# Attention over gathered rows: tying a body's gathers to the transposes of two bodies before

## The chip, the cores and the metric

The kernel runs on one core of one Trainium2 chip. The metric is the device time of one execution in microseconds (us), and a version is given by the median of its runs.

## What is computed

A graph of 6250 nodes and 100000 edges (sorted by receiving node) goes through a node update and two layers of attention over edges. The part that matters here is the attention of one layer:

```python
q = (x @ Wq + bq).reshape(n, H, C)          # n = 6250, H = 4, C = 32
k = (x @ Wk + bk).reshape(n, H, C)
v = (x @ Wv + bv).reshape(n, H, C)
e = (ea @ We).reshape(-1, H, C)             # 100000 edges
kj = k[src] + e
alpha = einsum('ehc,ehc->eh', q[dst], kj) / sqrt(C)
ex = exp(alpha - amax[dst])                 # softmax over the edges of a node
w = ex / (segment_sum(ex, dst)[dst] + 1e-16)
out = segment_sum((v[src] + e) * w, dst) + x @ Ws + bs
```

The kernel multiplies the projections into the queries beforehand, so that the attention works on the rows `x[src]` themselves: it gathers them, scores them against the queries of the receiving window, and sums the weighted rows.

## The kernel before

Edges are handled in tiles of 128. A **body** is four tiles (`QUAD`), and one attention stage has 224 bodies; there are two such stages, one for each layer (`attend_stage`). Each engine runs a loop whose round is eight bodies (`NS = 8`), written out body by body. All engines are coordinated by semaphores alone.

For body b the work is: SyncE loads the edge records of two bodies at a time (`part`, L1283), the queries and node codes of each body (L1305, L1306) and the edge codes (L1291). GpSimd gathers 4 x 128 rows of 128 floats by four indirect DMAs (L1326) into slot b mod 8 of the tile `ring`. TensorE turns the rows (`turn_rows`, L1340, four transposes) and puts the mask into the score bank (`mask_scores`, L1350). ScalarE copies the turned rows out of PSUM (`copy_rows`, L1411). TensorE scores them (`score`, L1358). VectorE finds the running maximum (L1460, L1463, L1467). ScalarE makes the weights (`weigh`, L1418, L1422). TensorE turns the weights (`turn_weights`, L1367), ScalarE copies them (`copy_weights`, L1429), TensorE multiplies them with the ring's rows (`gather_sums`, L1377) and VectorE adds the result to the sums (`add`, L1478).

The engines are staggered by hand. In step k TensorE does, in this order, the rows and mask of body k+2, the sums of body k, the scores of body k+2 and the weights' transposes of body k+1. ScalarE does `copy_rows` of k+2, `copy_weights` of k+1, `weigh` of k+2. VectorE does the small copy of k+2 (L1453), `add` of k, the maximum of k+2.

GpSimd has nothing else in these stages. Before the gathers of body b it waits for the edge records of b (`edge_in`) and for the sums of body b-8 (`summed`), which is when the slot of the ring is free again. So it may run up to six steps ahead of the transposes that read the rows. TensorE's matmuls signal `turned` (rows transposed), `scored`, `wt_ps` (weights transposed) and `summed`; counts that begin above zero are set by `sem_inc` at the start (L1391, L1392).

In the profile TensorE shows twice as many L1377, L1358 matmuls as the code writes, and L1340 and L1367 once each.

Of the kernel before, what the change touches and what calls it, by code (L numbers as in the profile page):

```python
# [33 lines left out]
NS = 8  # L34
# [167 lines left out]
def last_tiles(eng, m):  # L202

    return eng.value_load(m["atab"][0:1, 1, NWIN + 2:NWIN + 3], min_val=NWIN // TPR - 1, max_val=TCAP // TPR - 1)


def rounds(eng, m, step, begin=None, last_of=last_round, between=()):

    last, done = last_of(eng, m), 0
    for until, what in (*between, (last, None)):  # L210
        if what is None or until > done:
            with eng.Fori(done, until) as r:
                at = Round(eng, r)
                if begin:
                    begin(at, True)
                for k in range(NS):
                    step(at, k, NS)
        if what:
            what()
            done = until  # L220
    at = Round(eng, last)
    if begin:
        begin(at, False)
    for k in range(NS):
        step(at, k, NS - 1 - k)
# [986 lines left out]
def attend_stage(nc, m, layer):  # L1212
# [8 lines left out]
    with ExitStack() as c, ExitStack() as inner:  # L1221
# [36 lines left out]
        def xt_bank(k):  # L1258
            return bank[k % 2][:, 0:QE]

        def score_bank(k):
            return bank[2 + k % 2][:, 0:QE].rearrange("q (t e) -> q t e", t=QUAD)

        def wt_bank(k):
            return bank[4 + k % 2][:, 0:QE]

        def sum_bank(t):
            return bank[6 + t // 2][:, t % 2 * RW:(t % 2 + 1) * RW]

        def tiles_of(k, field, count=1):  # L1270
            here = field * NS + k % PART * QUAD * count
            return edge[:, k // PART, here:here + QUAD * count]

        def halves(at, c):
            return at.value(2 * NS, 2 * c)
# [39 lines left out]
        @block.gpsimd  # L1315
        def _(pool):
            pool.memset(codes[:, :, :, :], 1.0).then_inc(ready, 1)
            pool.memset(ring[:, :, :, FEAT:FEAT + 1], 1.0).then_inc(ready, 1)

            def step(at, k, left):  # L1320
                if k % PART == 0:
                    pool.wait_ge(edge_in[k // PART], at.turns(16, 0))
                pool.wait_ge(summed, halves(at, k + 1))
                pool.sem_inc(begun, 1)
                for t in range(QUAD):
                    pool.indirect_dma_start(  # L1326
                        out=ring[:, k, t, 0:FEAT], out_offset=None, in_=rows_of[:, :],
                        in_offset=bass.IndirectOffsetOnAxis(ap=tiles_of(k, 0)[:, t:t + 1], axis=0)
                        ).then_inc(rows_in[k], 16)

            rounds(pool, m, step, None, last_tiles)

        @block.tensor
        def _(pe):
            def turn_rows(at, body):

                k = body % NS
                pe.wait_ge(rows_in[k], at.turns(16 * QUAD, body))
                for t in range(QUAD):
                    last = pe.transpose(xt_bank(k)[:, t * P:(t + 1) * P], ring[:, k, t, 0:FEAT], ident[:, :])  # L1340
                last.then_inc(turned, 1)

            def mask_scores(at, body):

                k = body % NS
                pe.wait_ge(query_in[k % QS], at.value(2 * 64, 64 * (1 + body // QS)))
                pe.wait_ge(codes_in[k // PART], at.turns(16, body))
                for t in range(QUAD):

                    pe.matmul(score_bank(k)[:, t, :], nodes[:, k % QS, t, :], codes[:, k % QS, t, :], start=(t == 0),  # L1350
                              stop=False, skip_group_check=True)

            def score(at, body):

                k = body % NS
                pe.wait_ge(xt_there, at.body(body + 1))
                for t in range(QUAD):
                    last = pe.matmul(score_bank(k)[:, t, :], query[:, k % QS, t, :], x_t[k % 2][:, t * P:(t + 1) * P],  # L1358
                                     start=False, stop=True, skip_group_check=True)
                last.then_inc(scored, 1)  # L1360

            def turn_weights(at, body):

                k = body % NS
                pe.wait_ge(weighed, at.body(body + 1))
                for t in range(QUAD):
                    last = pe.transpose(wt_bank(k)[:, t * P:(t + 1) * P], weight[k % 2][:, t * P:(t + 1) * P], ident[:, :])  # L1367
                last.then_inc(wt_ps, 1)

            def gather_sums(at, k):  # L1370

                pe.wait_ge(wt_there, at.body(k + 1))
                pe.wait_ge(weights_in, at.body(k + 1))
                for half in (0, 2):
                    pe.wait_ge(added, at.value(NS * QUAD, QUAD * (k - 1 + NS) + half + 2))
                    for t in (half, half + 1):
                        last = pe.matmul(sum_bank(t), weight_t[k % 2][:, t * P:(t + 1) * P], ring[:, k, t, :], start=True,  # L1377
                                         stop=True)
                    last.then_inc(summed, 1)

            def step(at, k, left):
                if left >= 2:
                    turn_rows(at, k + 2)
                    mask_scores(at, k + 2)
                gather_sums(at, k)
                if left >= 2:
                    score(at, k + 2)
                if left >= 1:
                    turn_weights(at, k + 1)

            pe.sem_inc(summed, 2 * NS)  # L1391
            pe.sem_inc(scored, QS)  # L1392
            pe.wait_ge(ready, 5)
            begin = Round(pe, pe.snap(last_tiles(pe, m) * 0))
            for body in (0, 1):
                turn_rows(begin, body)
                mask_scores(begin, body)
                score(begin, body)
            turn_weights(begin, 0)
            rounds(pe, m, step, None, last_tiles)  # L1400

        @block.scalar
        def _(act):
            def copy_rows(at, body):

                k = body % NS
                act.wait_ge(turned, at.body(body + 1))
                if body >= 2:
                    act.wait_ge(scored, at.body(body - 1 + QS))
                    act.wait_ge(wt_ps, at.body(body - 1))  # L1410
                act.activation(x_t[k % 2][:, :], xt_bank(k), ACT.Copy).then_inc(xt_there, 1)  # L1411

            def weigh(at, body):

                k = body % NS
                act.wait_ge(shifted, at.body(body + 1 + NS))
                for t in range(QUAD):
                    last = act.activation(weight[k % 2][:, t * P:(t + 1) * P], score_bank(k)[:, t, :], ACT.Exp,  # L1418
                                          bias=run[:, k, t, STEPS - 1:STEPS])
                last.then_inc(weighed, 1)  # L1420
                act.wait_ge(changed, at.body(body + 1))
                act.activation(decay[:, k, :], change[:, k, :], ACT.Exp).then_inc(decayed, 1)  # L1422

            def copy_weights(at, body):

                k = body % NS
                act.wait_ge(wt_ps, at.body(body + 1))
                act.wait_ge(summed, halves(at, body - 1 + NS))
                act.activation(weight_t[k % 2][:, :], wt_bank(k), ACT.Copy).then_inc(wt_there, 1)  # L1429

            def step(at, k, left):
                if left >= 2:
                    copy_rows(at, k + 2)
                if left >= 1:
                    copy_weights(at, k + 1)
                if left >= 2:
                    weigh(at, k + 2)

            begin = Round(act, act.snap(last_tiles(act, m) * 0))
            copy_rows(begin, 0)  # L1440
            copy_rows(begin, 1)
            weigh(begin, 0)
            copy_weights(begin, 0)
            weigh(begin, 1)
            rounds(act, m, step, None, last_tiles)
# [500 lines left out]
```

## Time and profile before

| | us |
|---|---|
| median of 3 runs | 4399.23 |
| lowest, highest | 4367.18, 4400.29 |
| the profiled execution | 4405.89 |
| its span, first to last instruction | 4404.2 |
| granted TensorE clock, mean share of full | 0.775 |

The profile is of one execution. Its page gives busy times by engine, and views of the trace give groups of instructions, waits and an ordered list (the timeline). An engine row is the start in us from the start of the span, the duration, the engine, the line, the operation, tiles written<-read and the number merged; in brackets stands the idle time of the engine before it and what ended that. Of TensorE's matmuls the ends are modelled. "remote" is a wait whose release the profile could not assign to an instruction; "issue" is idle time before which nothing was waited for that the profile shows.

### The profile page before, as it was taken

What the parts mean: (1) busy time and instruction counts of PE and PEld (TensorE: products, weight loads), DVE (VectorE), ACT (ScalarE), POOL (GpSimd) and SP (SyncE); (2) the same over time, 40 slices, a digit from 0 to 9 for tenths busy, and PEclk for the clock granted to TensorE, in tenths of its full rate; (3) what the DMA queues carried; (4) which work ended last, traced back from release to release, by engine and by line L of the source; (5) the groups of instructions that cost most, each with busy time, mean ns of one, the idle gap of its engine ahead of it and who ended that gap; (6) DMA issues with size and microseconds to landing.
All of it is one profiled execution on the core that took longest, in us unless ns stands there. A gap on an engine that the chain in (4) does not pass through costs nothing. (4 is left out here: it accounts for less than half of the span.)

```text
span 4404.2 us, 85656 instructions
## 1 busy us (share of the span) xinstructions
PE 2949.7 (67%) x20523; PEld 2457.6 (56%) x20523; DVE 1843.2 (42%) x5924; ACT 1349.6 (31%) x4260; POOL 1920.7 (44%) x2203
## 2 busy tenths in 40 slices
PE   4567998466666666666667765666666666665676
PEld 2225998355555555555556544555565555555554
DVE  6464554233333333333335752333333333333357
ACT  1001443233333333333234432333333333332333
POOL 5200111555555555555552125555555555555522
PEclk5557999677777777777778987777777777777889
DMA  6985333232232223222233542222232223222220
GB/s 186 233 247 168 81 81 89 78 81 80 76 80 78 78 78 83 78 80 79 76 82 65 140 135 75 77 78 79 79 81 78 79 80 80 79 81 74 81 40 23
DMA packets 558920, 407.12 MB, mean 92 GB/s; under 512 B 229605, under 2 KB 526693, under 8 KB 558745
## 3 DMA queue, kind: packets, MB, share of 16 engines
q1 hardware_dynamic: 450840, 283.23, 22.9%
q0 software_dynamic: 58496, 122.80, 11.4%
q10 hardware_dynamic: 49536, 0.55, 0.6%
q8 instruction: 18, 0.29, 0.0%
q14 instruction: 30, 0.24, 0.0%
HBM read 333.73 MB, written 72.56 MB: 92 GB/s over the span
## 5 line engine op out<-in xcount | busy, mean ns | idle before, releaser
L1326 POOL DMA_INDIRECT a_ring<-xg,a_edge x1792 | 1690.3, 943 | 1498.8 <-issue 512.7
L1478 DVE SCALAR_TENSOR_TENSOR acc_all<-acc_all,a_decay,bank 128x130 f32 x1792 | 627.4, 350 | 1458.6 <-remote 906.5
L1377 PE MATMUL bank<-a_ring,a_weight_t 128*128 128x130 f32 x3584 | 684.4, 344 | 631.0 <-ACT a_weight_t L1429 330.5
L1358 PE MATMUL bank<-a_x_t,a_query 128*128 128x128 f32 x3584 | 707.7, 359 | 512.4 <-ACT a_x_t L1411 278.4
L1377 PEld LDWEIGHTS bank<-a_ring,a_weight_t 128*128 128x128 f32 x3584 | 571.6, 239 | 722.2 <-DVE acc_all L1478 359.0
L1358 PEld LDWEIGHTS bank<-a_x_t,a_query 128*128 128x128 f32 x3584 | 611.3, 257 | 593.1 <-ACT a_x_t L1411 320.9
L1429 ACT ACTIVATE a_weight_t<-bank 128x512 f32<-128x512 f32 x448 | 267.5, 597 | 1692.7 <-remote 777.8
L1418 ACT ACTIVATE a_x_t<-bank,a_run 128x128 f32<-128x128 f32 x1792 | 509.3, 371 | 271.2 <-DVE a_run L1463 211.4
L1460 DVE TENSOR_REDUCE a_bound<-bank 128x4 f32<-128x512 f32 x448 | 308.6, 689 | 424.3 <-issue 180.7
L1340 PE MATMUL bank<-ident,a_ring 128*128 128x128 f32 x1792 | 349.8, 331 | 37.3 <-DMA a_ring<-xg,a_edge 37.1
L1367 PE MATMUL bank<-ident,a_x_t 128*128 128x128 f32 x1792 | 364.1, 341 | 0.4 <-issue 0.4
L1411 ACT ACTIVATE a_x_t<-bank 128x512 f32<-128x512 f32 x448 | 273.9, 611 | 281.5 <-remote 210.6
L1340 PEld LDWEIGHTS bank<-ident,a_ring 128*128 128x128 f32 x1792 | 286.9, 179 | 38.5 <-DMA a_ring<-xg,a_edge 38.4
L1367 PEld LDWEIGHTS bank<-ident,a_x_t 128*128 128x128 f32 x1792 | 294.4, 183 | 0.7 <-issue 0.7
L517 PE MATMUL bank<-c_ring,c_onehot 128*32 128x128 f32 x2064 | 179.7, 400 | 123.7 <-DVE acc_all L479 92.7
L1350 PE MATMUL bank<-a_shared 17*128 17x128 bf16 x1792 | 202.3, 241 | 0.0
L517 PEld LDWEIGHTS bank<-c_ring,c_onehot 128*32 128x32 f32 x2064 | 70.6, 138 | 232.1 <-DVE acc_all L479 174.3
L1350 PEld LDWEIGHTS bank<-a_shared 17*128 17x128 bf16 x1792 | 114.3, 102 | 99.6 <-issue 99.6
L1453 DVE COPY a_ring<-a_edge 128x4 f32<-128x4 f32 x448 | 83.6, 187 | 181.3 <-issue 176.5
L1051 PE MATMUL bank<-x1t,w1x 128*128 (+1 forms) x784 | 157.9, 283 | 0.0
L471 DVE SCALAR_TENSOR_TENSOR c_onehot<-iota_n,wstart,c_node 128x96 f32<-128x96 f32 x344 | 108.5, 316 | 106.8 <-issue 76.6
L1052 PE MATMUL bank<-u_agg_t,w1a 128*128 128x128 f32 x784 | 152.8, 277 | 0.0
(258 smaller groups left out, 2778.6 us busy)
## 6 DMA issues: line engine op xcount, KB each, us to landing
a_query<-rec SPq DMA_DIRECT2D x896, 128.0 KB
c_ring<-in_edge_attr SPq DMA_DIRECT2D x344, 192.0 KB
a_ring<-xg,a_edge POOLq DMA_INDIRECT x1792
rec<-u_q_scores SPq DMA_DIRECT2D x98, 256.0 KB
rec<-p_q_scores SPq DMA_DIRECT2D x98, 256.0 KB
a_shared<-nrows SPq DMA_DIRECT2D x896, 8.5 KB
a_shared<-crows SPq DMA_DIRECT2D x224, 28.0 KB
c_node<-drec ACTq DMA_DIRECT2D x344, 1.5 KB
```

The source lines that it names most:

```text
L517: last = pe.matmul(sum_bank(k)[t * WN:(t + 1) * WN, 0:FEAT], onehot[:, k, t, :], ring[:, k, t, :], start=True, stop=True, tile_position=(0 ...
L1326: pool.indirect_dma_start(out=ring[:, k, t, 0:FEAT], out_offset=None, in_=rows_of[:, :], in_offset=bass.IndirectOffsetOnAxis(ap=tiles_of(k ...
L1340: last = pe.transpose(xt_bank(k)[:, t * P:(t + 1) * P], ring[:, k, t, 0:FEAT], ident[:, :])
L1350: pe.matmul(score_bank(k)[:, t, :], nodes[:, k % QS, t, :], codes[:, k % QS, t, :], start=(t == 0), stop=False, skip_group_check=True)
L1358: last = pe.matmul(score_bank(k)[:, t, :], query[:, k % QS, t, :], x_t[k % 2][:, t * P:(t + 1) * P], start=False, stop=True, skip_group_ch ...
L1367: last = pe.transpose(wt_bank(k)[:, t * P:(t + 1) * P], weight[k % 2][:, t * P:(t + 1) * P], ident[:, :])
L1377: last = pe.matmul(sum_bank(t), weight_t[k % 2][:, t * P:(t + 1) * P], ring[:, k, t, :], start=True, stop=True)
L1411: act.activation(x_t[k % 2][:, :], xt_bank(k), ACT.Copy).then_inc(xt_there, 1)
L1418: last = act.activation(weight[k % 2][:, t * P:(t + 1) * P], score_bank(k)[:, t, :], ACT.Exp, bias=run[:, k, t, STEPS - 1:STEPS])
L1429: act.activation(weight_t[k % 2][:, :], wt_bank(k), ACT.Copy).then_inc(wt_there, 1)
L1460: dve.tensor_reduce(bound[:, k, :, STEPS - 1:STEPS].rearrange("q t s -> q (t s)"), score_bank(k), AX.X, ALU.max, negate=True).then_inc(max ...
L1478: dve.scalar_tensor_tensor(here, here, decay[:, k, t:t + 1], sum_bank(t), ALU.mult, ALU.add).then_inc(added, 1)
```

## The change

GpSimd gets one wait more ahead of each body's gathers: on `turned`, so that the gathers of body b begin only when TensorE has turned the rows of body b-2. For this the count of `turned` begins at 8 (`NS`), and ScalarE's own wait on `turned` is raised by the same 8. The wait on `summed`, six steps older, stays. The number of DMAs, their sizes and all other orders are the same.

```diff
                 if k % PART == 0:
                     pool.wait_ge(edge_in[k // PART], at.turns(16, 0))
                 pool.wait_ge(summed, halves(at, k + 1))
+
+                pool.wait_ge(turned, at.body(k + NS - 1))
                 pool.sem_inc(begun, 1)
                 for t in range(QUAD):
                     pool.indirect_dma_start(
...
             pe.sem_inc(summed, 2 * NS)
             pe.sem_inc(scored, QS)
+            pe.sem_inc(turned, NS)
             pe.wait_ge(ready, 5)
...
                 k = body % NS
-                act.wait_ge(turned, at.body(body + 1))
+                act.wait_ge(turned, at.body(body + 1 + NS))
```

## Rows read from the trace of the kernel before

**Rows 1.** The page: busy time, share of the span and instructions of each engine.

```profile
PE 2949.7 (67%) x20523; PEld 2457.6 (56%) x20523; DVE 1843.2 (42%) x5924; ACT 1349.6 (31%) x4260; POOL 1920.7 (44%) x2203
```

**Rows 2.** Both attention stages by windows: busy us (x instructions), PEclk, DMA share, GB/s.

```profile
774.60:2386.00 1611.40, 1044.82 (x6228) 909.26 (x6228) 574.06 (x1771) 508.07 (x1556) 845.20 (x896) 0.74 0.30 79
2632.00:4242.00 1610.00, 1030.85 (x6228) 896.03 (x6228) 573.51 (x1773) 505.77 (x1555) 839.41 (x891) 0.76 0.30 78
```

**Rows 3.** First stage by line: duration ns min/median/max, first and last start us.

```profile
L1340 PE MATMUL bank<-ident,a_ring x896: 272/273/476, 781.8 to 2386.0; 128*128 128x128 f32 x180
...
L1326 POOL DMA_INDIRECT a_ring<-xg,a_edge x896: 938/944/1052, 774.6 to 2363.9; - x180
```

**Rows 4.** GpSimd's waits, whole span: us in total, times, longest us.

```profile
POOL a_ring L1326 <- issue: 512.7, 1535, 1.7
POOL a_ring L1326 <- DMA a_edge<-trec: 442.1, 94, 10.7
POOL a_ring L1326 <- PE bank L1377: 430.4, 107, 5.6
...
POOL a_ring L1326 <- remote: 113.6, 56, 2.5
```

**Rows 5.** Timeline of the first stage's beginning: the first, the eighth gather, TensorE, ScalarE.

```profile
774.65 1.05 POOL L1326 DMA_INDIRECT a_ring<-xg,a_edge  x1 [1.98 <-DMA a_edge<-trec]
...
781.78 1.12 PE L1340 MATMUL bank<-ident,a_ring 128*128 128x128 f32 x4 [18.10 <-DMA a_ring<-xg,a_edge]
...
783.51 0.94 POOL L1326 DMA_INDIRECT a_ring<-xg,a_edge  x1 [0.30 <-issue]
...
786.04 1.11 PE L1340 MATMUL bank<-ident,a_ring 128*128 128x128 f32 x4 [0.39 <-DMA a_ring<-xg,a_edge]
...
800.84 0.60 ACT L1411 ACTIVATE a_x_t<-bank 128x512 f32<-128x512 f32 x1 [17.31 <-issue]
```

**Rows 6.** Timeline with GpSimd in groups of four gathers (first or last of each shown).

```profile
825.06 0.94 POOL L1326 DMA_INDIRECT a_ring<-xg,a_edge  x1 [10.64 <-DMA a_edge<-trec]
...
828.81 0.94 POOL L1326 DMA_INDIRECT a_ring<-xg,a_edge  x1 [0.30 <-issue]
...
829.20 0.60 PE L1367 MATMUL bank<-ident,a_x_t 128*128 128x128 f32 x4
...
831.07 0.60 ACT L1429 ACTIVATE a_weight_t<-bank 128x512 f32<-128x512 f32 x1 [2.92 <-PE bank L1367]
831.61 0.94 POOL L1326 DMA_INDIRECT a_ring<-xg,a_edge  x1 [1.86 <-remote]
...
834.57 1.16 PE L1358 MATMUL bank<-a_x_t,a_query 128*128 128x128 f32 x8 [1.61 <-issue]
...
836.00 0.60 PE L1340 MATMUL bank<-ident,a_ring 128*128 128x128 f32 x4
...
837.13 0.94 POOL L1326 DMA_INDIRECT a_ring<-xg,a_edge  x1 [0.83 <-issue]
...
844.11 0.94 POOL L1326 DMA_INDIRECT a_ring<-xg,a_edge  x1 [2.29 <-remote]
```

**Rows 7.** Timeline with eight gathers in a row (the first and the eighth shown).

```profile
3008.10 0.94 POOL L1326 DMA_INDIRECT a_ring<-xg,a_edge  x1 [5.51 <-DMA a_edge<-trec]
...
3011.47 0.60 PE L1367 MATMUL bank<-ident,a_x_t 128*128 128x128 f32 x4
...
3016.84 0.94 POOL L1326 DMA_INDIRECT a_ring<-xg,a_edge  x1 [0.30 <-issue]
...
3018.92 0.60 ACT L1429 ACTIVATE a_weight_t<-bank 128x512 f32<-128x512 f32 x1 [8.62 <-remote]
```

**Rows 8.** TensorE's timeline at the stage's end, after the last gather.

```profile
2370.34 2.08 PE L1358 MATMUL bank<-a_x_t,a_query 128*128 128x128 f32 x8 [0.67 <-ACT a_x_t L1411]
...
2373.06 1.06 PE L1340 MATMUL bank<-ident,a_ring 128*128 128x128 f32 x4
...
2385.65 0.60 PE L1340 MATMUL bank<-ident,a_ring 128*128 128x128 f32 x4
```

## The prediction, made before the changed kernel was run

> **What bounds the kernel now.** I read the page first. No engine is near full: TensorE 67%, its weight loads 56%, GpSimd 44%, VectorE 42%, ScalarE 31% [rows 1]. So the time is in waits, and a mean over stages will not say which. The windows of the two attention stages come next: 1611 and 1610 us, together 73% of the 4404 us span, with TensorE busy 65% and GpSimd 52% of each, and DMA engines 30% [rows 2]. The change touches only these.
>
> In a stage the transposes of the rows start once for each body, the first at 781.8 and the last body's at 2385.7, so 223 steps take 1603.9 us: 7.19 us a step [rows 3, 8]. What could a step be? After the last gather (begun at 2363.9) the steps go on alone: from the transposes at 2373.06 to those at 2385.65 it is three steps, 4.20 us each [rows 3, 8]. So three microseconds of each step are there only while GpSimd gathers.
>
> Next, who waits for what while it gathers. Four gathers start 1.25 us apart: 825.06 to the end of the fourth at 829.75 is 4.69 us [rows 6]. TensorE ends its transposes of weights at 829.80, and ScalarE, which has nothing else to wait for (the sums that it needs too are older), starts the copy at 831.07: 1.27 us late, 1.32 us after GpSimd's last gather ended [rows 6]. In a run of eight the same hand-over takes much longer: transposes end at 3012.07, GpSimd goes on to 3017.78, ScalarE starts at 3018.92, 6.85 us late and 1.14 us after GpSimd stopped [rows 7]. At the stage's beginning, where GpSimd gathers without a pause, transposes that end at 787.15 reach ScalarE at 800.84, 13.7 us late [rows 5]. My reading: a signal of TensorE that falls in the later part of a run of gathers is delivered only after the run, some 1.2 us behind its end; the longer the run, the longer the hold. The profile has no name for it (it says "remote" or "issue"), so this is an inference from three hand-overs.
>
> How often are runs long? GpSimd starts 1792 gathers, 1535 of them without a real wait (0.33 us each) and 94 + 107 + 56 = 257 after one [rows 4]. There are 448 bodies, so 191 bodies, three of seven, follow the one before without a pause: the runs of eight. The ring's lead, and edge records that come for two bodies at a time (94 waits of 4.7 us on them), make them. The real waits add up to 442.1 + 430.4 + 113.6 = 986 us, 2.20 us a body; with 4 x 1.25 us that is the 7.2 us of a step again. So now: bursts of 9.7 us that hold TensorE's signals, then a pause in which edge records and sums catch up.
>
> **The change part by part.** The counts that begin at 8, `sem_inc` and ScalarE's raised constant, cost one instruction a stage: nothing. The new wait is one sequencer instruction a body on GpSimd, which does nothing but gathers here; behind it stand that body's four gathers, and behind them TensorE's transposes of the body. SyncE's queue is not touched.
>
> *Are the rows late then?* The gathers of b start when the rows of b-2 are turned, and are needed two steps later. From start to use in the trace: the eight gathers begin at 774.65, the last ends at 784.45, and the transposes that need it start at 786.04, 1.6 us later [rows 5]. So 0.15 (the wake, an estimate: half of the 0.30 us that lie between two gathers [rows 7]) + 4.69 + 1.6 = 6.4 us against two steps of more than 8.4 us even at 4.2 us a step. Covered; at the step forecast below the cover is twice the need. The cover is gone only if landing took over 6 us. On this the Trainium skill, "DMA: Bandwidth & Descriptors", section "Anatomy of one DMA", would put the fixed part of a GpSimd DMA at about 2.0 us plus bytes/436e3, 2.15 us for 64 KB; the sum would be 7.0 us, also covered, and the first row has it shorter, 1.6 us. The same page, "Rules for kernel authors", advises to issue a DMA early and wait late, which speaks against giving up lead; by it the change could at best do nothing, and I keep that as a rival.
>
> *What runs become.* GpSimd's next start needs the signal `turned` of a body, and this signal is itself one of those held until the run is over. So after each four gathers there must be a pause: runs of eight vanish. The pause is at least 1.3 us (the hold's tail) plus the wake 0.15: 4.69 + 1.45 = 6.15 us from one run to the next, if TensorE has done the transposes by then. It has when its clock is at 2.4 GHz: the release lets ScalarE start at 831.07, the scores start at 834.57 and the transposes of the next rows end at 836.60, 5.6 us after the release [rows 6]. So **6.15 us** a step. At 1.2 GHz the eight score matmuls take 2.08 instead of 1.16 us, the transposes of rows 1.06 instead of 0.60 [rows 6, 8], and those of the weights as much again: 5.6 + 0.9 + 0.45 + 0.45 = **7.4 us**. But in such a step the weights are signalled ahead of the next run and the following step gains that, so I take every second one at 7.4: (7.4 + 6.15)/2 = 6.8 us. The clock is granted at 0.74 and 0.76 [rows 2], half of the time at each level: (6.15 + 6.8)/2 = **6.45 us** a step. A stretch of the trace in which three runs of four follow each other agrees: 825.06 to 844.11 is 19.05 us for three steps, 6.35 us [rows 6].
>
> *The beginning of a stage.* Bodies 0 and 1 are gathered at once as before, body 2 when the rows of 0 are turned (782.90, while the eight gathers still run): twelve gathers in a row, to 784.45 + 5.0 = 789.5. The signal at 787.15 that came at 800.84 now comes at 789.5 + 2 = 791.7 at the latest. From there 222 steps.
>
> *The sum.* Last transposes of the stage at 791.7 + 222 x 6.45 = 2223.6 instead of 2385.7: 162 us less. What comes after (two more steps) is the same, as GpSimd is done by then in either. The second stage has the same length and counts: 2 x 162 = 324 us. The profiled execution took 4405.9 us (span 4404.2): 4082 us; it stood 6.7 us above the median, so **4075 us**.
>
> Bounds of the step: 6.15 throughout (clock always full) gives 791.7 + 1365 = 2157, 458 us less in all, 3941 us. 6.8 throughout gives 791.7 + 1510 = 2301, 168 us less, 4231 us. 7.4 throughout would be 97 us more, 4496 us.
>
> **Rivals.**
> *No change.* The hold goes by gathers, not by runs: each body costs its 5.0 us and 2.2 us of hand-overs whatever the grouping. For it: runs of eight and of four seem to share one mean, 2.20 us of real wait a body [rows 4]; and the advice above. Against it: the three steps of 6.35 us [rows 6]. Then only the stage's beginning is gained, at most some 13 us of it in each: 4370 to 4400 us.
> *Slower: the sums are held too.* After a release the weights are copied by 0.7 us and the eight matmuls of L1377 end 1.9 us (2.4 GHz) to 2.9 us (1.2 GHz) behind it, and GpSimd's run is then two to three microseconds old. If the hold begins that early, VectorE's `add` waits for the release, and its 1.8 us, ahead of the maximum in its queue, pass into the chain: 5.6 + 1.8 = 7.4 us at full clock, 9.2 at half, 8.3 on average; 791.7 + 222 x 8.3 = 2634, 497 us more in all, 4896 us. It decides from the point at which the hold starts less than 2 to 3 us into a run. Against it: in the same four-gather stretch the step stayed at 6.35 us.
> *Slower: rows late.* If gathers land over 6 us behind their issue while SyncE loads 79 GB/s [rows 2], every second step waits. Each us beyond is half a us a step, 224 us in all; with 2 us beyond, 4850 us. The 1.6 us of [rows 5], with SyncE busy as well, speaks against it.
> *The wait does nothing.* TensorE's `turned` of b-2 might always be there earlier. It can't: GpSimd starts a body four steps after its present earliest point.
>
> **Numbers.** Forecast 0.70 (its own range 3940 to 4235), no change 0.14, sums held 0.10, rows late 0.03, and 0.03 for still faster, where shorter stalls keep the clock up and the hold's tail is shorter. A measurement here can tell about 1% (44 us) from no change. Faster by over 1%: 0.73; within 1%: 0.14; slower: 0.13. The range goes from 3930 to 4400 us: forecast and most of "no change".
>
> **What the profile after would show.** The gathers' waits: about 445 instead of 257, by TensorE's L1340, and the edge-record waits gone, since these come steps ahead. Steps of 6.2 to 6.8 us between transposes. ScalarE's waits for "remote" before L1429 down from many to few microseconds. Transposes waiting for DMA no more than at the beginnings. I am wrong if the steps stay at 7.2 with a pause after each four gathers (the hold is per gather), or if TensorE waits for the ring.

## The result and the profile after

The changed kernel takes 4116.57 us in the median of four runs (4108.88 to 4127.3) against 4391.39 for the kernel before, measured beside it: a ratio of 0.939, with an interval of 0.935 to 0.944. The profiled execution took 4127.3 us, its span 4125.6. The lines of the changed kernel that matter here stand two or three further down: gathers L1328, transposes of the rows L1342, scores L1360, transposes of the weights L1369, sums L1379, copy of the rows L1414, copy of the weights L1432, `add` L1481.

The page's line of busy times, and both attention stages by windows (length, busy us of PE, PEld, DVE, ACT, POOL, then PEclk, DMA share, GB/s):

```profile
PE 2862.7 (69%) x20523; PEld 2379.6 (58%) x20523; DVE 1836.7 (45%) x5924; ACT 1339.6 (32%) x4260; POOL 1925.4 (47%) x2203
```

```profile
774.60:2245.00 1470.40, 989.72 (x6225) 859.59 (x6226) 571.52 (x1776) 503.57 (x1559) 846.29 (x895) 0.79 0.33 86
2490.00:3960.00 1470.00, 993.78 (x6206) 863.56 (x6207) 569.05 (x1768) 499.82 (x1554) 843.38 (x892) 0.78 0.33 86
```

VectorE, ScalarE and GpSimd have the busy time of [rows 1, 2], TensorE 55 and 37 us less, as its clock stands at 0.79 and 0.78 instead of 0.74 and 0.76. Everything else that went was idle time inside the two stages. (A higher clock alone does not bring the gain: `sum4`, below, has the highest clock of all kernels on its chip, 0.818 over its span against 0.803 for the changed kernel, and is within 1% of the kernel before.) How much of it, and that nothing came from anywhere else, the transposes of the rows show (duration min/median/max in ns, first and last start; one line for each stage):

```profile
L1342 PE MATMUL bank<-ident,a_ring x896: 272/273/477, 780.6 to 2245.6; 128*128 128x128 f32 x180
```

```profile
L1342 PE MATMUL bank<-ident,a_ring x896: 272/273/475, 2491.5 to 3963.6; 128*128 128x128 f32 x180
```

The first stage's last row is turned 140 us earlier than in [rows 3], the second's 278 us (4241.8 before); the span is 278.6 us shorter. The step is (2245.6 - 780.6) / 223 = 6.57 us, and 6.60 in the second stage, against 7.2 before.

GpSimd's waits (us in total, times, longest), to be held against [rows 4]:

```profile
POOL a_ring L1328 <- issue: 467.5, 1434, 2.1
POOL a_ring L1328 <- remote: 460.6, 208, 3.1
POOL a_ring L1328 <- PE bank L1342: 314.6, 134, 3.7
...
POOL a_ring L1328 <- PE bank L1379: 4.6, 15, 0.3
POOL a_ring L1328 <- DMA a_edge<-trec: 2.1, 1, 2.1
```

The edge records cost 2.1 us instead of 442.1, the sums 4.6 instead of 430.4. In their place stands the new wait, 775.2 us under two names. Together 782 us / 448 = 1.75 us a body, where it was 2.20. The waits for TensorE's signals on the other engines are in no group of rows of before (there the copy of the weights waited 777.8 us for "remote", 135 times, and `add` 906.5 us, 199 times). Now they are:

```profile
ACT a_weight_t L1432 <- remote: 971.9, 170, 7.8
ACT a_weight_t L1432 <- PE bank L1369: 699.3, 250, 4.4
DVE acc_all L1481 <- remote: 641.4, 163, 9.2
...
PE bank L1342 <- DMA a_ring<-xg,a_edge: 83.7, 53, 19.1
```

Two runs of gathers in the timeline of the changed kernel, one of eight and one of four:

```profile
1201.32 0.95 POOL L1328 DMA_INDIRECT a_ring<-xg,a_edge  x1 [1.79 <-remote]
...
1204.36 1.06 PE L1342 MATMUL bank<-ident,a_ring 128*128 128x128 f32 x4
...
1206.32 0.95 POOL L1328 DMA_INDIRECT a_ring<-xg,a_edge  x1 [0.30 <-issue]
...
1207.95 0.60 PE L1369 MATMUL bank<-ident,a_x_t 128*128 128x128 f32 x4
...
1208.38 0.60 PE L1342 MATMUL bank<-ident,a_ring 128*128 128x128 f32 x4
...
1210.08 0.95 POOL L1328 DMA_INDIRECT a_ring<-xg,a_edge  x1 [0.30 <-issue]
...
1212.95 0.60 ACT L1432 ACTIVATE a_weight_t<-bank 128x512 f32<-128x512 f32 x1 [6.05 <-remote]
...
1213.70 0.95 POOL L1328 DMA_INDIRECT a_ring<-xg,a_edge  x1 [2.68 <-remote]
...
1217.45 0.94 POOL L1328 DMA_INDIRECT a_ring<-xg,a_edge  x1 [0.30 <-issue]
...
1221.97 0.94 POOL L1328 DMA_INDIRECT a_ring<-xg,a_edge  x1 [3.58 <-PE bank L1342]
```

The weights are turned by 1208.55, the run ends at 1211.03, ScalarE starts at 1212.95: 4.40 us late, 1.92 us behind the run. GpSimd's own `turned` of 1208.98 is held as well and lets it go at 1213.70. So the mechanism of the forecast is there. But the run of eight is there too: the transposes that end at 1205.42, four microseconds into the run, got their signal out in time for the fifth gather at 1206.32. Not every signal that falls into a run is held.

Counted over all gathers, with a run ended by a pause of 1.2 us or more (and a lone gather with the seven behind it, 1.7 us apart, taken as one run of eight), the first stage had 90 runs of eight and 33 of four before, and has 53 and 115 now. A pause after a run of eight shrank from 4.3 to 2.6 us on average, one after a run of four from 2.8 to 2.15. The shorter pauses are the whole gain. A body in a run of eight cost (9.70 + 4.27) / 2 = 6.99 us before, one that is a run of its own 4.69 + 2.82 = 7.51; at these prices the new mixture of runs would cost (106 x 6.99 + 115 x 7.51) / 221 = 7.26 us a body, no less than before.

### The profile page after: what moved, and what is told of

Its sections match the earlier page's. It is cut to its first block and busy times, and to the rows that moved or that the text cites. A ratio compares the mean times of both kernels' runs of the same rounds, so it can differ in the third digit from the quotient of the medians.

```text
span 4125.6 us, 86106 instructions
## 1 busy us (share of the span) xinstructions
PE 2862.7 (69%) x20523; PEld 2379.6 (58%) x20523; DVE 1836.7 (45%) x5924; ACT 1339.6 (32%) x4260; POOL 1925.4 (47%) x2203
## 5 line engine op out<-in xcount | busy, mean ns | idle before, releaser
L1328 POOL DMA_INDIRECT a_ring<-xg,a_edge x1792 | 1694.9, 946 | 1249.3 <-issue 467.5
L1481 DVE SCALAR_TENSOR_TENSOR acc_all<-acc_all,a_decay,bank 128x130 f32 x1792 | 627.1, 350 | 1326.6 <-remote 641.4
L1379 PE MATMUL bank<-a_ring,a_weight_t 128*128 128x130 f32 x3584 | 665.1, 340 | 692.4 <-ACT a_weight_t L1432 534.0
L1379 PEld LDWEIGHTS bank<-a_ring,a_weight_t 128*128 128x128 f32 x3584 | 563.2, 238 | 770.2 <-DVE acc_all L1481 398.2
L1432 ACT ACTIVATE a_weight_t<-bank 128x512 f32<-128x512 f32 x448 | 267.5, 597 | 1756.6 <-remote 971.9
L1360 PE MATMUL bank<-a_x_t,a_query 128*128 128x128 f32 x3584 | 675.4, 347 | 213.2 <-issue 108.1
L1360 PEld LDWEIGHTS bank<-a_x_t,a_query 128*128 128x128 f32 x3584 | 582.4, 247 | 290.5 <-issue 149.1
L1342 PE MATMUL bank<-ident,a_ring 128*128 128x128 f32 x1792 | 331.7, 317 | 85.3 <-DMA a_ring<-xg,a_edge 83.7
L1369 PE MATMUL bank<-ident,a_x_t 128*128 128x128 f32 x1792 | 343.8, 326 | 0.4 <-ACT a_x_t L1421 0.4
L1342 PEld LDWEIGHTS bank<-ident,a_ring 128*128 128x128 f32 x1792 | 263.7, 169 | 100.3 <-DMA a_ring<-xg,a_edge 98.1
L1414 ACT ACTIVATE a_x_t<-bank 128x512 f32<-128x512 f32 x448 | 276.2, 616 | 94.0 <-remote 49.3
L1369 PEld LDWEIGHTS bank<-ident,a_x_t 128*128 128x128 f32 x1792 | 278.8, 175 | 0.8 <-ACT a_x_t L1421 0.7
L1161 POOL COPY x<-u_xs 128x128 f32 (+1 forms) x49 | 14.3, 291 | 299.8 <-DVE u_xs L1195 299.8
```

Source lines behind the costliest of these rows:

```text
L1328: pool.indirect_dma_start(out=ring[:, k, t, 0:FEAT], out_offset=None, in_=rows_of[:, :], in_offset=bass.IndirectOffsetOnAxis(ap=tiles_of(k ...
L1481: dve.scalar_tensor_tensor(here, here, decay[:, k, t:t + 1], sum_bank(t), ALU.mult, ALU.add).then_inc(added, 1)
```

## The experiments

Three theories stood against each other. **H**, the forecast's: TensorE's signals are held in runs of gathers, and the new wait helps since it is on such a signal and so breaks the runs (in the expectations of the first four runs this is R, in the short form that runs of eight are what costs). **E**: the gain is the edge records' 442 us, which any lesser lead gives back. **L**: the lead itself, or a wait once a body on whatever signal. Beside them stand P, that the point of TensorE's step at which the gathers begin matters, and whether the gathers' bytes are at work. All times are medians; a ratio is to the kernel before on the same chip.

The experiments ran on three chips. The kernel before took 4382.39 us on the first and 4409.04 us on the third, and 3422.86 us on the second. What that means is told with the runs of the second chip. Line numbers shift by one to five from kernel to kernel.

**Breaking all runs by another wait (`land`).** The kernel before, where a body's gathers wait until those of the body before have landed:

```diff
                 pool.wait_ge(summed, halves(at, k + 1))
+                if k:
+                    pool.wait_ge(rows_in[k - 1], at.turns(16 * QUAD, k - 1))
                 pool.sem_inc(begun, 1)
```

> The kernel before (lead of the ring kept at eight bodies), but GpSimd waits for the landing of the previous body's gathers before the next body's, at seven of eight bodies: no run of eight gathers is left, and 1.6 us or more lie between runs of four. Theory R (runs of eight are what costs: breaking them up is what the change brought): a step of 6.4 to 6.6 us, about 4110 us, ratio 0.94. Theory E (what went is GpSimd's waiting for edge records at its largest lead; the grouping of gathers costs nothing): the pause fits into the 2.2 us that GpSimd waits for a body anyway, ratio 0.99 to 1.01, and the waits on edge records stay at some 300 to 440 us.

Measured: 4296.1 us, 0.981 (0.977 to 0.984). GpSimd's and TensorE's waits:

```profile
POOL a_ring L1328 <- issue: 1317.2, 1584, 4.6
...
POOL a_ring L1328 <- DMA a_ring<-xg,a_edge: 97.4, 201, 2.9
```

```profile
PE bank L1342 <- DMA a_ring<-xg,a_edge: 788.2, 342, 18.6
```

The runs are broken (27 of eight, 170 of four in a stage), and the edge records no longer count, yet only a third of the gain comes. The pause came out at 2.5 us instead of the 1.6 planned: GpSimd needs 4.69 + 2.5 = 7.2 us for a body that is a run of its own (the step is 6.97) and is now the bound, with TensorE waiting 788 us for rows. Both expectations missed. The run speaks against E (edge waits down to 3.8 us, gain not there), though not cleanly, since it brought a bound of its own.

**The new wait for every second body only (`pair2`).** The changed kernel with

```diff
-                pool.wait_ge(turned, at.body(k + NS - 1))
+                if k % PART == 0:
+                    pool.wait_ge(turned, at.body(k + NS - 1))
```

> The changed kernel with its new wait only before every second body, so that gathers come in runs of eight throughout while the lead stays at two to three bodies and edge records are there in time. Theory R: the step returns to about 7.2 us, about 4380 us, ratio 0.99 to 1.0. Theory E: a run of eight costs 9.7 us and a pause of 2.7 us, 12.4 to 13.2 us for two bodies, as in the changed kernel: 4080 to 4150 us, ratio 0.93 to 0.945.

Measured: 4560.68 us, 1.040 (1.035 to 1.044).

```profile
POOL a_ring L1329 <- PE bank L1343: 1122.7, 197, 8.5
```

The waits for edge records are 2.0 us, as small as in the changed kernel, the lead is the same within a body, and it is slower than before. E falls, and so does the lead as a cause. R had the direction, but its 0.99 to 1.0 was too low. What differs is that all gathers go in runs of eight (110 in a stage) with 5.3 to 5.4 us between them: (9.70 + 5.35) / 2 = 7.5 us a step, and 7.54 is measured. One correction to H shows here as well: where the weights are turned two to four microseconds into the run, ScalarE's copy is late in 147 of 170 bodies, by 2.5 us in the median, but starts while the run still goes on. A hold often ends before the run does.

**A wait on the sums instead (`sum4`).** The kernel before with its `summed` wait four bodies tighter, `halves(at, k + 5)`, and no wait on `turned`.

> The kernel before with its own wait on the sums tightened from body b-8 to body b-4, and no wait on the turned rows: nearly the same lead as the change, by a signal that TensorE sends some 2 us later in its step. Theory R and theory E: as the change, ratio 0.935 to 0.95. Theory P (it matters at which point of TensorE's step the gathers begin): more than 1.5% away from the change in either direction, 4180 us or more, or 4050 us or less.

Measured: 4343.65 us, 0.992 (0.989 to 0.995).

```profile
POOL a_ring L1326 <- PE bank L1377: 760.1, 177, 9.8
```

```profile
PE bank L1340 <- DMA a_ring<-xg,a_edge: 385.4, 272, 18.6
```

Less lead, edge waits of 3.9 us, and one wait a body, also on a signal of TensorE; but 73 runs of eight stay in the first stage, with 4.8 us behind each, and TensorE waits 385 us for rows that come late. Both R and E had 0.935 to 0.95 and missed; P has it. Which signal is waited for matters. How much of it is the late rows stays open: `sum6`, made to tell, ran only on the second chip, where it could not.

**The new wait with three bodies more of lead (`lead5`).** The changed kernel with `at.body(k + NS - 4)`: the gathers of b wait for the rows of b-5.

> The changed kernel with the wait on the rows turned five bodies ago instead of two: GpSimd keeps most of its lead, and is still paced by a signal of each body. Theory R: as the change, but five bodies gathered in a row at each stage's start: 4110 to 4150 us. Theory E: the same where edge records come in time at a lead of five, 4110 to 4150 us; if they don't, some 100 to 200 us of waits on edge records and 4200 to 4300 us.

Measured: 4139.2 us, 0.944 (0.941 to 0.948).

```profile
POOL a_ring L1328 <- remote: 377.4, 177, 5.6
POOL a_ring L1328 <- PE bank L1342: 269.5, 130, 3.6
POOL a_ring L1328 <- PE bank L1379: 65.5, 17, 4.4
POOL a_ring L1328 <- DMA a_edge<-trec: 41.0, 17, 3.7
```

All but the whole gain (0.939) with five bodies of lead instead of two. R and E both had this time, so it does not part them. Giving up lead brings nothing in itself; it is the wait on `turned` that works.

**The second chip: no hold, no effect.** On it four kernels ran: `xt5`, `sum6` (the kernel before, `summed` two bodies tighter), `short` and `split3` (the same kernels as `xt5_b`, `short_b` and `split3_b` below).

> As the run with the rows turned five bodies ago (4139 us, ratio 0.944), but GpSimd waits for ScalarE's signal that the turned rows of body b-5 are copied, instead of TensorE's signal that they are turned. Same lead, one signal a body, edge records in time as there; ScalarE's signals show no hold. Theory H (a pause behind each run comes about because TensorE's signal is itself held until the run is over): runs of eight in number again, as before or more, a step of 7.0 to 7.3 us, ratio 0.97 to 1.01. Theory L (any signal once a body will do, since what was lost before were the waits on edge records): as with TensorE's signal, ratio 0.94 to 0.95.

> The kernel before with GpSimd's wait on the sums moved from body b-8 to b-6, two bodies more of lead than in the run with b-4 (ratio 0.992), where TensorE waited 385 us for rows. Theory late rows (that run was slow since rows came late, not by its signal): without late rows it reaches the change, ratio 0.94 to 0.95. Theory H: half of the bodies come in runs of eight again whatever the lead, since the sums' signal comes early enough in a step to get through; a step near 7.0 us, ratio 0.98 to 1.0.

> The kernel before with rows of 32 floats gathered instead of 128 (the other 96 columns of the ring are set once to 1; the results are meaningless, the work of all engines is the same): same number of gathers and descriptors, a quarter of the bytes. If the bytes that gathers move hold TensorE's signals back: holds shrink, step under 6.5 us, ratio under 0.93. If it is the making of descriptors or their number: ratio 0.99 to 1.01.

> The change with a lead of three, and a second wait in the middle of each body's four gathers, on the scores of body b-3, which TensorE finishes some 3 us after the rows: runs of two gathers where the signal comes late, of four else. Theory H: two gathers (2.2 us) are too short to hold a signal, so holds shrink: a step of 5.6 to 6.3 us, 3880 to 4040 us, ratio 0.885 to 0.92. If the hold depends on GpSimd's share alone or the second wait costs as much as it gives: 0.94 or more.

Measured: 3422.06, 3423.91, 3424.58 and 3422.33 us, ratios of 1.0000, 1.0004, 1.0008 and 1.0004, each within 0.002. None moves anything, whatever the theory. The trace of `xt5` there shows why. Its first attention stage by windows, GpSimd's and TensorE's waits, and a piece of its timeline:

```profile
773.00:1893.00 1120.00, 831.52 (x6224) 708.67 (x6225) 567.83 (x1773) 518.64 (x1555) 840.96 (x891) 0.93 0.43 113
```

```profile
POOL a_ring L1327 <- issue: 544.1, 1780, 1.9
```

```profile
PE bank L1341 <- DMA a_ring<-xg,a_edge: 575.0, 373, 18.8
```

```profile
1195.50 0.60 PE L1368 MATMUL bank<-ident,a_x_t 128*128 128x128 f32 x4
1196.21 0.60 ACT L1431 ACTIVATE a_weight_t<-bank 128x512 f32<-128x512 f32 x1 [1.99 <-PE bank L1368]
1196.29 0.95 POOL L1327 DMA_INDIRECT a_ring<-xg,a_edge  x1 [0.30 <-issue]
1197.54 0.94 POOL L1327 DMA_INDIRECT a_ring<-xg,a_edge  x1 [0.30 <-issue]
```

GpSimd gathers without one pause from the stage's first body to its last, and ScalarE still gets the weights 0.11 us after they are turned, in the middle of it. Gathers take the same 0.94 us each, 1.25 us from one to the next; the step is 4 x 1.25 = 5.0 us, and TensorE waits for rows. So on this chip the kernel is bound by GpSimd, and the stage lasts 1120 us instead of 1611. The gathers themselves take no longer on the other chips; what differs in the traces is that there TensorE's signals come late. TensorE's clock differs too (0.93 granted here, 0.74 there, which is 213 us of TensorE's busy time in a stage), and no run parts the two, so not all of the 490 us need be the hold. This is strong support for the hold itself, which here is missing altogether. It also means that the result of 0.939 belongs to chips that hold. What the changed kernel itself does on this one was not measured; the four runs make no difference likely.

Three of the four kernels (not `sum6`) were run again on the third chip, together with the changed kernel.

**The changed kernel on the third chip (`again`).**

> The changed kernel itself once more. The runs before this one showed that chips differ: on one the kernel before takes 4382 us and TensorE's signals are held back while GpSimd gathers, on another it takes 3422 us, GpSimd gathers without a pause at 5.02 us a body and nothing is held. On a chip of the first kind: ratio 0.935 to 0.945 as first measured. On one of the second kind: rows of body b-2 are turned 2.9 us before the gathers of b begin in any case, so the new wait never waits: ratio 0.998 to 1.002.

Measured: 4150.62 us, 0.942 (0.938 to 0.946), step 6.64 us; it repeats, with fewer runs of eight (37 in the first stage instead of 53).

**A wait on ScalarE's copy of the rows (`xt5_b`).** The same lead as `lead5`, but on the signal that ScalarE gives when it has copied the rows, in the median 2.7 us after they are turned:

```diff
+                pool.wait_ge(xt_there, at.body(k + NS - 4))
...
-                pe.wait_ge(xt_there, at.body(body + 1))
+                pe.wait_ge(xt_there, at.body(body + 1 + NS))
...
+            pe.sem_inc(xt_there, NS)
```

> GpSimd paced by ScalarE's signal for body b-5, as before; the first time the chip held nothing back, so it could not tell. On a chip that holds: theory H (the pause is made by TensorE's held signal) ratio 0.97 to 1.01 with runs of eight as often as before; theory L (any signal once a body will do) 0.94 to 0.95. On a chip that does not: 1.0.

Measured: 4625.73 us, 1.049 (1.044 to 1.055): the slowest of all. Its timeline, with the gathers that begin and end a four:

```profile
1196.08 0.94 POOL L1327 DMA_INDIRECT a_ring<-xg,a_edge  x1 [6.01 <-ACT a_x_t L1413]
...
1199.82 0.94 POOL L1327 DMA_INDIRECT a_ring<-xg,a_edge  x1 [0.30 <-issue]
1199.96 0.62 ACT L1413 ACTIVATE a_x_t<-bank 128x512 f32<-128x512 f32 x1
1201.39 0.94 POOL L1327 DMA_INDIRECT a_ring<-xg,a_edge  x1 [0.63 <-issue]
...
1201.75 0.60 PE L1368 MATMUL bank<-ident,a_x_t 128*128 128x128 f32 x4
...
1205.13 0.94 POOL L1327 DMA_INDIRECT a_ring<-xg,a_edge  x1 [0.30 <-issue]
1207.74 0.60 ACT L1431 ACTIVATE a_weight_t<-bank 128x512 f32<-128x512 f32 x1 [7.16 <-remote]
...
1209.72 0.61 ACT L1413 ACTIVATE a_x_t<-bank 128x512 f32<-128x512 f32 x1
1211.14 0.94 POOL L1327 DMA_INDIRECT a_ring<-xg,a_edge  x1 [5.07 <-ACT a_x_t L1413]
```

This settles L: one wait a body, with the lead of `lead5`, and the result is on the other side of 1, beyond H's 0.97 to 1.01 too. ScalarE's signal is not held while GpSimd gathers: the next gather starts 0.81 us after ScalarE's copy ends, at 1200.58 during a four as at 1210.33 during a pause. So the next four start 0.63 us after the last, in the middle of TensorE's step; the weights turned at 1202.35 are 1.0 us into the new four and reach ScalarE 5.39 us later, 1.67 us after its end. In a run of its own a signal so early passes (all 24 in the first microsecond of a four of the kernel before); two fours with 0.63 us between them act on it as one run of eight. The short pause does not hold back everything, though: of the sums' first halves that such a first four holds, half reach `add` 1.1 to 1.5 us behind its end, when the second has begun, while most of the second halves come only behind the second. Of the pauses between bodies 137 (both stages) are between 0.5 and 0.7 us. Counted as everywhere here, by pauses of 1.2 us, a stage has some 107 runs of eight and none of four, and the step of 7.68 us is near the 7.54 of `pair2`. Counted by unbroken gathers alone there would be a third as many runs of eight, no more than in `lead5`; H's count needs the timeline's reading of the short pause.

**A quarter of the bytes (`short`, `short_b`).** The kernel before, where each gathered row has 32 of its 128 floats: `in_=rows_of.rearrange("n (a f) -> (n a) f", a=4)` into `ring[:, k, t, 0:FEAT // 4]`; the other 96 columns are set to 1 once, so the kernel leaves out three quarters of each row. The expectation for `short_b`:

> Rows of 32 floats instead of 128 in every gather (results meaningless, work of all engines the same). On a chip that holds: bytes as the cause give under 0.93, making of descriptors as the cause gives 0.99 to 1.01. On a chip that does not: 1.0, as measured.

Measured: 4414.63 us, 1.0004 (0.998 to 1.003). Its first attention stage by windows has TensorE busy for the same time as [rows 2] with 52 GB/s instead of 79:

```profile
774.60:2386.00 1611.40, 1041.21 (x6161) 906.29 (x6162) 568.08 (x1757) 503.69 (x1541) 847.53 (x897) 0.74 0.22 52
```

The waits are those of before, 88 to 92 runs of eight a stage among them. The bytes moved are no part of the cause. That leaves the number of gathers, or what GpSimd does to issue them; no run tells these apart.

**Shorter runs still (`split3_b`).** The changed kernel with a lead of three bodies instead of two, and each body's gathers split two and two, the second pair waiting for the scores of three bodies ago:

```diff
-                pool.wait_ge(turned, at.body(k + NS - 1))
+                pool.wait_ge(turned, at.body(k + NS + 1 - 3))
                 pool.sem_inc(begun, 1)
                 for t in range(QUAD):
+                    if t == 2:
+                        pool.wait_ge(scored, at.body(k - 2 + QS))
+                        pool.sem_inc(begun, 1)
```

> Lead of three and a second wait between a body's second and third gather. On a chip that holds: theory H 0.885 to 0.92, else 0.94 or more. On a chip that does not: 1.0, as measured.

Measured: 4113.0 us, 0.933 (0.929 to 0.937), beside 4150.62 for the changed kernel on the same chip. GpSimd's and VectorE's waits:

```profile
POOL a_ring L1331 <- remote: 646.0, 348, 3.9
...
POOL a_ring L1331 <- PE bank L1363: 158.2, 92, 2.4
```

```profile
DVE acc_all L1484 <- remote: 169.9, 76, 5.9
```

It is the best version measured on chips that hold, and neutral on the other (1.0004), but 38 us are far from the 0.885 to 0.92 expected. `add` waits less for "remote" (169.9 us, where the changed kernel on this chip has 476.1), GpSimd as much as ever: 804 us against 814. The scores, which were late at VectorE 77 times in the changed kernel, are late 260 times. Finer runs move the hold from one signal to another more than they remove it. As two things were changed, how much of the 38 us is the split and how much the lead of three is not shown.

**The late signals of every trace.** One more count can be made from the traces alone. Take five hand-overs of TensorE in each of the 448 bodies: rows and weights to ScalarE, scores and both halves of the sums to VectorE (GpSimd's own waits are not among them). How often did the receiving engine sit idle for more than 0.6 us after the signalling matmul had ended, out of 2240, and for how long in all?

| kernel | us | late signals | idle us behind them |
|---|---|---|---|
| `split3_b` | 4113.0 | 727 | 1388 |
| the changed kernel | 4116.57 | 473 | 1484 |
| `lead5` | 4139.2 | 469 | 1505 |
| `again` | 4150.62 | 505 | 1405 |
| `land` | 4296.1 | 417 | 811 |
| `sum4` | 4343.65 | 569 | 1744 |
| the kernel before | 4391.39 | 577 | 1796 |
| `short_b` | 4414.63 | 563 | 1767 |
| `pair2` | 4560.68 | 626 | 2113 |
| `xt5_b` | 4625.73 | 697 | 2555 |
| `xt5`, second chip | 3422.06 | 2 | 1 |

But for `land`, whose bound is GpSimd, and for neighbours in the list, the time follows the last column. The same count over three hand-overs of ScalarE and VectorE (copied rows and copied weights to TensorE, the maximum to ScalarE), 1344 in each trace, finds none late in any kernel on any chip. And of the weights turned more than 1.5 us after a run of gathers had ended, none reached ScalarE late (46 in the kernel before, 26 in the changed one). So, as far as these counts go, it is TensorE's signals alone that are late, and only around gathers.

## Why the prediction was right, and where it was not

**The mechanism: right in that there is a hold, too strict in its rule.** The forecast read from three hand-overs that TensorE's signals are held while GpSimd gathers, and delivered only behind the run [rows 5, 6, 7]. In the trace of the changed kernel, of the 105 copies of the weights whose signal falls more than five microseconds into a run of eight, 102 start behind the run's end, 84 of them 1.7 to 2.1 us behind it; on the second chip the hold is missing. But the rule does not hold in general. The third hand-over itself speaks against it: the run of gathers in which ScalarE starts at 800.84 [rows 5] goes on to 814.42, 10.64 us before the gather at 825.06 [rows 6]. In the kernel before, of 121 such copies only 86 start behind the run, and 14 are late by less than 0.6 us; in `pair2` 30 of 59 do. Nor are early signals safe: of the weights turned more than two microseconds into a run of four in the changed kernel, 31 of 134 are late by less than 0.6 us, 52 by more but still inside the run, 51 come behind it.

**The beginning: right, and to the digit by luck.** Twelve gathers in a row, as forecast, then the signal that came at 800.84 [rows 5], forecast for 791.7 at the latest:

```profile
787.02 0.95 POOL L1328 DMA_INDIRECT a_ring<-xg,a_edge  x1 [0.30 <-issue]
...
790.17 0.60 ACT L1414 ACTIVATE a_x_t<-bank 128x512 f32<-128x512 f32 x1 [7.86 <-remote]
```

The stage began 1.53 us earlier than before (first gather at 773.12 instead of 774.65), so this is 791.70 in the time of before. The gathers end where the forecast had them (787.97, which is 789.50). What is behind them is 2.20 us, for which the forecast wrote 2 without a row; and 789.5 + 2 is 791.5, not 791.7.

**The step: near, 6.57 and 6.60 for 6.45, and this is the whole miss.** From 790.17 to the last body's transposes at 2244.9 there are 222 steps of 6.55 us; in the second stage, from the same copy at 2501.78, 6.58. With 0.10 and 0.13 us too little in 444 steps the forecast is 52 us short by this term; its span was 4404.2 - 324 = 4080 us, the measured one 4125.6, 45 us more.

**What made the step: partly wrong.** The forecast had every run of eight vanish, because the signal waited for would itself be held. They went from 90 to 53 in the first stage. And the pause after a four was put at 1.45 us, or what TensorE needs at its lower clock; it is 2.15, and still 1.82 in the 114 of 227 cases where the rows waited for were turned before the run had ended. The two misses nearly cancel, and that is luck: fours alone would have given 6.84 us a step. A body that is a run of its own costs 4.69 + 2.15 = 6.84 us; two in a run of eight cost 9.70 + 2.63 = 12.33 us, 6.17 each; 115 of the one and 106 of the other give 6.52 us. So the mean came out near 6.45, but not from the steps of 6.15 and 7.4 us that it was made of: half of the steps lie under 5.3 us, a quarter over 8.3. That the clock is at each level half of the time (0.79 and 0.78 granted) did no harm to the sum.

That a body in a run of eight could be cheaper than one in a four was not seen, though it is so in the kernel before as well (6.99 against 7.51 us). It depends on what stands behind the run, and this the traces show. In the changed kernel the second four starts without a pause only if the `turned` it waits for is out, that is when TensorE is ahead; then the rows that the next run waits for are turned before the run ends too (104 of 105 runs of eight, 2.3 us before the end on average), and all that follows is the delivery of that signal, 2.6 us. In `pair2` the second four starts whether TensorE is ahead or not; there these rows are turned only after the run in 198 of 218 cases, 4.1 us after its end on average, and the pause is 5.3 us. In `xt5_b`, likewise, the copy waited for ends 4.5 us behind the run, and the pause is 5.35 us. So long runs cost little here since they happen only where TensorE's work is already done, and the 6% do not come from there being none. Why the pause after a four shrank as well, from 2.8 to 2.15 us, no run parts: the waits for edge records and for sums went from it together.

**The signs.** Edge records' waits gone: right (442.1 to 2.1 us). New waits about 445: 342, as 90 bodies follow without one and 15 waits go by another name. ScalarE's waits for "remote" down from many to few: wrong, they rose from 777.8 to 971.9 us; what fell is GpSimd's waits taken together (986 to 782 us) and VectorE's for "remote" (906.5 to 641.4). Transposes waiting for rows at the beginnings only: nearly, 53 waits with 83.7 us where there were 3 with 37.1 (nearly all of which are the two beginnings), so some 45 us of the profile are rows that came a little late. The forecast's 6.4 us from one body's `turned` to the use of the gathered rows took 0.15 us for the wake, though the signal is itself held: in the trace GpSimd starts 2.1 us after the rows are turned where a run of four went before, and 4.9 us after where it was one of eight. And its 1.6 us counts from the end of the last gather's time on GpSimd; from that gather's start, at 783.51, to the use at 786.04 it is 2.5 us [rows 5].

**The rivals.** "No change" fell with the step. "The sums are held too" was right in that they are (641.4 us), wrong in that it would decide: they were held more before. "Rows late" is the 45 us above and not more. (The 79 GB/s that it puts down to SyncE are all DMA traffic; `short_b`, with a quarter of the gathered bytes, has 52.) The Trainium skill's advice in "DMA: Bandwidth & Descriptors", section "Rules for kernel authors", to issue early and wait late, is harmless here and not the point: `lead5` with five bodies of lead and the changed kernel with two differ by half a per cent or less.

**Open.** Why chips differ, what in GpSimd's issuing of gathers holds TensorE's signals, which signals of a run are held and what ends a hold inside it, and how much of the second chip's shorter time is the missing hold and how much TensorE's higher clock. No run here tells.

## What to carry to other kernels

When an engine is late by microseconds behind work that had long ended, look at what the other engines do in that time before adding buffers or lead: here signals were late only while GpSimd issued gathers or up to 1.5 us behind, and a pause placed by the late signal itself was worth 6%, one of another length or on another signal between a gain of 2% and a loss of 5%. Waiting on the consumer's own progress makes a long run happen only when the consumer is ahead; a fixed grouping does not, and cost 4%. And run such a change on more than one chip: this one is worth 6% on chips that hold, and its relatives nothing at all on one that doesn't.

## What the hardware showed that was not expected

- Chips of the same kind differ by a fifth on the same kernel: 3422.86 us against 4382.39 and 4409.04. In the traces from the faster chip (of four close relatives of that kernel) all of it lies in the two attention stages, whose gathers begin at 766 to 777 us everywhere. TensorE's granted clock is also higher there, 0.90 to 0.91 over the span against 0.76 to 0.82.
- Where signals are held they are held long: for some 6 us in a run of eight, while the same hand-over takes 0.11 to 0.12 us on the chip that doesn't hold. ScalarE's and VectorE's signals are late on neither (0 of 1344 by more than 0.6 us in each trace).
- What is held to a run's end mostly comes 1.0 to 1.4 us behind a run of four and 1.6 to 2.3 us behind a run of eight ([rows 7], with 1.14 us, is one of the exceptions). A pause of 0.6 us between two fours lets part of it out.
- An indirect gather of 128 rows takes GpSimd 0.94 us, and 1.25 us with what lies between two, whether the rows have 512 or 128 bytes.
